# Work moved out of the routing blocks: turned tiles copied a step later, eight row buffers, router logits by groups, and the first expert weight slots split inside the normalisation before each mixture

## What is computed

```python
def _layernorm(x, axis=-1, eps=1e-05):
    m = jnp.mean(x, axis=axis, keepdims=True)
    v = jnp.var(x, axis=axis, keepdims=True)
    return (x - m) / jnp.sqrt(v + eps)
...
    x = x + _L0_ffn_ref(_layernorm(x, axis=-1), ...)   # logits = x @ Wg, softmax, top 2 of 8
    ...
    x = x + _L1_ffn_ref(_layernorm(x, axis=-1), ...)   # logits = x @ gate_w.T, sigmoid + bias, top 4 of 16
```

## Time and profile before

| what | us |
|---|---|
| median of 3 runs (lowest, highest) | 1519.88 (1517.51, 1522.65) |
| the profiled execution | 1531.23 |
| its span from first to last instruction | 1529.2 |
| boundary and route ahead of the first mixture | 517.8 to 575.3 |
| boundary and route ahead of the second mixture | 1099.4 to 1189.4 |

### The profile page before, as it was taken

One profiled execution on the slowest core, in us unless ns is written; L12 is line 12 of the kernel. 1 busy time (PEld: TensorE's weight loads), 2 busy tenths in 40 slices (PEclk: granted clock), 3 DMA queues, 4 the chain that ended last, 5 costly groups with the idle time before them and its releaser, 6 DMA issues. The chain is left out here.

```text
span 1529.2 us, 41178 instructions
## 1 busy us (share of the span) xinstructions
PE 1169.9 (77%) x13430; PEld 862.1 (56%) x13430; DVE 1031.0 (67%) x2885; ACT 826.0 (54%) x2163; POOL 435.7 (28%) x480
## 2 busy tenths in 40 slices
PE   4899999998798539999999927678723327787890
PEld 2688888886344429988888724235611215555660
DVE  5699999997647777966666545345779228454566
ACT  6688888885588546844444306127454125444450
POOL 0555555551200000023333202000200641555550
PEclk9999999999899759999999958789955659899895
DMA  2333333331000283011111169970160320222228
GB/s 95 99 78 80 82 76 81 81 82 64 1 1 1 91 318 155 2 57 47 51 50 51 37 204 321 348 234 1 66 255 28 87 65 19 73 76 78 78 69 281
DMA packets 111934, 151.45 MB, mean 99 GB/s; under 512 B 13632, under 2 KB 96960, under 8 KB 111680
## 3 DMA queue, kind: packets, MB, share of 16 engines
q1 hardware_dynamic: 95792, 114.11, 23.6%
q0 software_dynamic: 11328, 30.95, 6.6%
q10 hardware_dynamic: 4688, 4.72, 0.9%
HBM read 127.97 MB, written 21.76 MB: 98 GB/s over the span
## 5 line engine op out<-in xcount | busy, mean ns | idle before, releaser
L1291 ACT ACTIVATE mixture_and_attentions_h<-ps,mixture_and_attentions_b 128x128 f32<-128x128 f32 x440 | 125.3, 373 | 137.3 <-PE ps L1243 134.3
L1243 PE MATMUL ps<-xture_and_attentions_m_w 128*128 128x128 f16 x1872 | 156.2, 219 | 1.8 <-DVE xture_and_attentions_m_w L1319 1.7
L1243 PEld LDWEIGHTS ps<-xture_and_attentions_m_w 128*128 x1872 | 129.1, 98 | 37.1 <-issue 3.5
L648 POOL TENSOR_TENSOR ads_and_recurrence_ctx_s<-ads_and_recurrence_ctx_c,ads_and_recurrence_ctx_s 128x512 f16<-128x512 f32 x64 | 74.2, 1159 | 178.2 <-ACT ads_and_recurrence_ctx_s L577 178.2
L597 ACT ACTIVATE ads_and_recurrence_probs<-ps,s_and_recurrence_neg_max 128x257 f32<-128x257 f32 x256 | 117.7, 480 | 1.1 <-DVE s_and_recurrence_neg_max L679 1.1
L1261 PE MATMUL ps<-xture_and_attentions_m_w,ixture_and_attentions_hs 128*128 x312 | 117.5, 379 | 1.0 <-DVE xture_and_attentions_m_w L1344 1.0
L1599 POOL DMA_INDIRECT tage_second_mixture_rows<-n_rows,e_second_mixture_r_token x79 | 76.8, 973 | 133.7 <-POOLq L1002 110.0
L1475 PE MATMUL ps<-stage_second_mixture_m_w,stage_second_mixture_x_s 128*128 x474 | 98.5, 348 | 20.7 <-ACT stage_second_mixture_x_s L1517 13.9
L1603 POOL DMA_INDIRECT y_rows<-stage_second_mixture_y,ge_second_mixture_r_dest x79 | 77.1, 976 | 124.6 <-DVE stage_second_mixture_y L1571 114.5
L1371 POOL DMA_INDIRECT ture_and_attentions_rows<-n_rows,e_and_attentions_r_token x39 | 39.0, 999 | 258.1 <-POOLq L1002 159.6
L1327 DVE TENSOR_SCALAR ixture_and_attentions_hs<-mixture_and_attentions_h 128x512 f16<-128x512 f32 x110 | 47.6, 433 | 87.7 <-PE ps L1262 71.3
(11 more groups left out here) (401 smaller groups left out, 3371.9 us busy)
## 6 DMA issues: line engine op xcount, KB each, us to landing
ads_and_recurrence_ctx_t<-in_ctx_t SPq DMA_DIRECT2D x64, 257.0 KB, 2.7
e_and_attentions_b_ctx_t<-in_ctx_t SPq DMA_DIRECT2D x15, 1028.0 KB, 9.1
ure_and_attentions_b_ctx<-in_ctx SPq DMA_DIRECT2D x30, 512.0 KB, 8.9
xture_and_attentions_m_w<-in_m_w SPq DMA_DIRECT2D x2, 5632.0 KB, 37.3
ds_and_recurrence_mask_i<-in_mask SPq DMA_DIRECT2D x256, 32.1 KB, 1.7
tage_second_mixture_rows<-y_rows SPq DMA_DIRECT2D x16, 512.0 KB, 9.6
stage_second_mixture_m_w<-in_m_w SPq DMA_DIRECT2D x2, 3840.0 KB, 20.5
xture_and_attentions_m_w<-in_m_w SPq DMA_DIRECT2D x1, 5120.0 KB, 16.6
```

The costliest lines, as they stand in the source:

```text
L1243: last = pe.matmul(ps[:, UB + 2 * (u % 2) + f // PER, (f % PER) * P:(f % PER + 1) * P], slots.of(e, c, at, P), a[:, c, :], start=(n == 0), ...
L1291: last = act.activation(h32[n][:, at:at + P], ps[:, UB + 2 * (u % 2) + n, at:at + P], ACT.Silu, scale=1 / (WS * NS), bias=b1[:, bass.ds(e ...
```

## The change

Only boundaries with `rows=True` and what belongs to them are changed. ACT copies a pair of turned tiles one step later, and PE has four PSUM banks for them in place of two. There are eight row buffers in place of four, with eight semaphores for their stores. The logits are computed in the boundary, four tiles at a time, in the place where other boundaries have their projections (after the turns of steps 3, 5, 7 and 9). The first slots are split inside the boundary, on ACT in steps 5 to 8 and on DVE in steps 6 to 8 with one behind the last step. In the second mixture `early` falls from 5 to 3, so two more slots are split among the tiles: 14 slots over 12 tiles, two slots after tile 5 and two after tile 11.

```diff
-    PB, TB = 0, 2
+    PB, TB, AHEAD = (0, 0, 4) if b.rows else (0, 2, 2)
+    RB = 8 if b.rows else 4
...
             def turn(t):
                 pe.wait_ge(k.l_low.sem, k.l_low.at(t + 1))
-                pe.wait_ge(k.l_turned.sem, k.l_turned.at(t - 1))
-                out = ps[:, TB + t % 2, 0:D].bitcast(F16)
+                pe.wait_ge(k.l_turned.sem, k.l_turned.at(t - AHEAD + 1))
+                out = ps[:, TB + t % AHEAD, 0:D].bitcast(F16)
...
-                act.wait_ge(k.l_turn.sem, k.l_turn.at(t - 3))
-                if b.rows and t >= 4:
-                    act.wait_ge(k.x_rows[t % 4].sem, k.x_rows[t % 4].at(t // 4))
+                act.wait_ge(k.l_turn.sem, k.l_turn.at(t - RB + 1))
+                if b.rows and t >= RB:
+                    act.wait_ge(k.x_rows[t % RB].sem, k.x_rows[t % RB].at(t // RB))
...
-                if 0 < s <= H:
+                if b.rows and 1 < s <= H + 1:
+                    turned(2 * s - 4)
+                    turned(2 * s - 3)
+                if not b.rows and 0 < s <= H:
                     turned(2 * s - 2)
                     turned(2 * s - 1)
+                if b.slots and 5 <= s < 5 + b.slots.mix.early:
+                    b.slots.cast_high(act, s - 5)
...
+                if b.slots and 6 <= s < 6 + b.slots.mix.early:
+                    b.slots.cast_low(dve, s - 6)
+            if b.slots:
+                for i in range(H - 5, b.slots.mix.early):
+                    b.slots.cast_low(dve, i)
...
-MIX1 = Mixture(1, E1, K1, 1, 2 * C * I1 + 2 * D, P, 5, (3, 5, 11, 17), 1.0)
+MIX1 = Mixture(1, E1, K1, 1, 2 * C * I1 + 2 * D, P, 3, (3, 5, 11, 17), 1.0)
...
+def logits(k, mix, wg):
+    def project(pe, g, part):
+        if part == 0:
+            for t in range(4 * g, 4 * g + 4):
+                products = [(w, x, c) for w, x in three(wg, (k.n_h, k.n_l)) for c in range(C)]
+                for n, (w, x, c) in enumerate(products):
+                    last = pe.matmul(k.ps[:, 7, t * mix.E:(t + 1) * mix.E], x[:, c, t * P:(t + 1) * P], w[:, c, :], start=(n == 0), stop=(n == len(products) - 1))
+            if g == G - 1:
+                last.then_inc(k.m_logits.sem, 1)
+    return project
...
         def _(act):
-            for i in range(mix.early):
-                slots.cast_high(act, i)
             scores(act)
...
-            for i in range(mix.early):
-                slots.cast_low(dve, i)
             choose(dve)
...
         def casts(u):
-            return range(mix.early + u, mix.early + u + 1) if mix.early + u < mix.count else ()
+            rest, tiles = mix.count - mix.early, NT - 4
+            return range(mix.early + rest * u // tiles, mix.early + rest * (u + 1) // tiles) if u < tiles else ()
```

More of the change, by code:

```diff
@@ L1034, in _ @@
         def _(pe):
-            for t in range(NT):
-                products = [(w, x, c) for w, x in three(wg, (k.n_h, k.n_l)) for c in range(C)]
-                for n, (w, x, c) in enumerate(products):
-                    last = pe.matmul(ps[:, LB, t * E:(t + 1) * E], x[:, c, t * P:(t + 1) * P], w[:, c, :], start=(n == 0), stop=(n == len(products) - 1))
-            last.then_inc(k.m_logits.sem, 1)
             pe.wait_ge(k.m_counted.sem, k.m_counted.at(1))
@@ L1682, in stage_first_mixture_and_attentions @@
             slots = Slots(k, mix, ctx)
-            boundary(k, Boundary(weights, rows=True, fetch=fetch_ahead))
+            boundary(k, Boundary(weights, project=logits(k, mix, k.w["L0_ffn_Wg"]), rows=True, fetch=fetch_ahead, slots=slots))
             route_first(k, mix, slots, r)
@@ L1719, in choose @@
                 dve.tensor_tensor(r.w[:, n, :], ex[:, :, n], z[:, 3, :], ALU.mult)
-        route(k, mix, k.w["L0_ffn_Wg"], slots, scores, choose, r)
+        route(k, mix, slots, scores, choose, r)
 class Ring:
@@ L2142, in stage_second_mixture @@
             slots = Slots(k, mix, ctx)
-            boundary(k, Boundary(weights, rows=True, fetch=lambda sp: slots.fetch(sp, (0,))))
+            boundary(k, Boundary(weights, project=logits(k, mix, k.w["L1_ffn_gate_w_t"]), rows=True, fetch=lambda sp: slots.fetch(sp, (0,)), slots=slots))
             route_second(k, mix, slots, r)
@@ L2363, in build @@
         k.t_raw = [k.count(f"t_raw{p}", unit=16) for p in range(4)]
-        k.x_rows = [k.count(f"x_rows{p}", unit=16) for p in range(4)]
         k.ctx_t_loaded = [k.count(f"ctx_t{p}", unit=16) for p in range(Ring.SLOTS)]
@@ L2367, in build @@
         k.g_load = [k.count(f"g_load{p}", unit=16) for p in range(4)]
+        k.x_rows = [k.count(f"x_rows{p}", unit=16) for p in range(4)] + k.g_load
         k.t_rows = [k.count(f"t_rows{p}", unit=16) for p in range(8)]
```

34 lines of the change are left out of this document (17 added, 17 removed).

## The result

| | kernel before | changed kernel |
|---|---|---|
| median of 20 runs each | 1523.83 us | 1512.22 us |
| lowest, highest | 1517.51, 1529.71 | 1502.51, 1518.71 |
| ratio | 1 | 0.9927 (95% interval 0.9910 to 0.9944) |
| profiled execution (its span) | 1531.23 (1529.2) | 1517.76 (1515.8) |

The change saves 11.1 us, 8.5 to 13.7. The forecast was -11.2 us. The kernel before now has more runs and a median 4 us above the one that the prediction started from, so the difference is compared and not the absolute time.

A forecast was written before the change was run, and what follows sets the result against it. The prediction took DVE to set the boundaries' pace, with slots and a transfer wait delaying the route blocks. It summed -4.85 - 9.2 + 2.8 = -11.2 us, from 1519.9 to 1508.7 us, range 1501 to 1517.

The forecast's parts named there:

- Boundary steps: In both boundaries: steps without DVE's wait take 2.28 us in place of 2.54, and ACT's store wait costs nothing.
- End of the boundary: ACT's last copies and PE's logits, not the store, close the boundaries, 0.4 us later in the first, 0.2 in the second.
- the delay by the first slot: First boundary, steps 5 and 6: ACT ends its first slot 4.1 us after step 5 starts, making low 5.3, not 4.6.
- First route block: First mixture: DVE has only its constants left, 0.55 us, before reading the logits, in place of 5.80; 5.25 us saved.
- Second route block: Second mixture: DVE's first choice step comes 1.75 us in, in place of 11.17; 9.4 us saved.
- Two extra slots: Second tile block, tiles 5 and 11 behind the gathers: each extra slot costs 1.40 us of DVE, 2.8 us lost.
- Gathers: Head of second tile block: 44 gathers take the same 55 us, two slots under them, and engines resume as they end.
- 0.3 us for each slot: Second tile block: a slot's DVE work under the gathers delays a gather by 0.3 us; unchanged in number, adding nothing.
- (a): Rival, boundary: high, low and slot halves wait for each other, 7.6 us back, 1516.3 us; chance 0.10.
- (b): Rival, gather stretch: two tile periods fall behind it, 1514.2 us (chance 0.12), or two more under it, 1501.8 (further 0.10).
- (c): Rival: stall behind gathers grows as instructions arrive later; slower above 11.2 us of additional wait; chance 0.05.
- (d): Rival, boundaries: eight buffers or the later copy bring nothing, as waits only move; 1514.7 us; chance 0.03.

The follow-up runs named there:

- e1: Kernel before with only the later copies of turned tiles and the eight row buffers; 1515.92 us, ratio 0.9951.
- e3: Changed kernel with the early slots split at the head of the route blocks again, logits still in the boundary; 1516.80 us, ratio 0.9958 to the kernel before.
- e2: Kernel before with only early 3 in place of 5 in the second mixture and its 14 slots over 12 tiles; 1522.78 us, ratio 0.9994.
- e8: Kernel before, unchanged, profiled a second time; 1530.92 us.
- e11: Kernel before with later copies, eight buffers and gathers paced by DVE's results, 12 ahead; 1425.05 us, ratio 0.9943, kernel before 1434.48 on that chip.
- e4: Changed kernel with the old order: copies in their own step, two banks, four row buffers; 1525.19 us against 1524.13 of the kernel before.
- e5: Changed kernel with 24 gathers in a row in place of 44, the other 55 later; 1521.14 us against 1530.23 of the kernel before, ratio 0.9946.
- e6: Changed kernel with 44 gathers, after the first 12 POOL waiting for PE before every second one; 1493.60 us against 1530.23 of before, ratio 0.9757.
- e12: Changed kernel with gathers paced by DVE's results, six ahead, rerun on a slower chip; 1486.61 us against 1528.40 of the kernel before, ratio 0.9727.
- e9: Changed kernel with gathers paced by DVE's results, 12 ahead, two per tile; 1420.31 us, ratio 0.9902, kernel before 1434.48 on that chip.
- e10: Changed kernel with gathers paced by DVE's results, six ahead, mean 2.4 per tile; 1419.64 us, ratio 0.9896, kernel before 1434.48 on that chip.

## Why the prediction was right, point by point

**Boundary steps.** 2.28 us forecast, 2.27 measured, without the wait for the store. With the order alone this is worth 4.2 and 4.1 us (e1), of which my sum never wrote a number, because it priced only the end with the slots. The slots and the logits take 3.9 and 3.8 of it back (changed kernel against e1).

**End of the boundary.** The closing by ACT's copies and PE's logits was right, the size was not: -0.3 twice in place of +0.4 and +0.2. The term that was too large is the delay by the first slot. The working has ACT done with it 4.1 us behind the step's start and the low half 0.7 late; ACT was done after 3.9 (529.62 to 533.50), since its copies and slots take 0.95 each, and DVE waited 0.46. What follows was carried along: the last low half ended at 541.0 where the working gives 541.6.

**First route block.** DVE read the logits 0.33 us in, not 0.55; the saving was 5.4 for 5.25. e3 shows that the slots on DVE were the whole of it and the place of the logits none.

**Second route block.** 1.71 us for 1.75, and 9.5 for 9.4. e2 splits it: 5.3 from early 3 (two slots and the transfer), 4.2 from moving the other three. Against e8's 62.7 us it is 8.4 and 4.2: how long the kernel before waits for the transfer varies.

**Two extra slots.** Right in place, the size in doubt. Their tile periods are 4.2 us (results of tiles 5 and 6 at 1246.7 and 1250.9), the pair on DVE is one row:

```profile
1265.02 2.88 DVE L976 SCALAR_TENSOR_TENSOR stage_second_mixture_m_w<-stage_second_mixture_m_w 128x1280 f16<-128x1280 f32 x2
...
1268.11 2.10 PE L1492 MATMUL ps<-stage_second_mixture_m_w,stage_second_mixture_x_s 128*128 x6 [4.12 <-DVE stage_second_mixture_m_w L976]
```

and PE's wait for the last slot grew from 2.8 to 4.1. On the chips with the stall the kernels that have them fall 2.9 to 6.7 us short of their stages, so +2.8 is at the low end; what could cost more than twice 1.4, the traces do not say. From the first profile of before, the other terms are -15.5 where the sum had -14.0, and the two errors nearly cancel; from the second they are -14.0, and the change falls short by 2.9, both as forecast. The runs do not decide between the two, and the measured gain has an interval of 8.5 to 13.7 us: that 11.2 met 11.1 so closely is luck either way.

**Gathers.** 44 of them in 55.5 us, as forecast. Three slots of ACT stood under them, not two, and two of DVE. The prediction lets the engines resume as the gathers end; a tile's result came 4.4 us behind the last gather's start, and 7.6 in the kernel before. The two gathers that started under DVE's slots took 1.20 and 1.29 us, the others 0.95 to 1.04:

```profile
1189.34 0.95 POOL L1616 DMA_INDIRECT tage_second_mixture_rows<-n_rows,e_second_mixture_r_token  x1 [0.30 <-issue]
1190.59 1.20 POOL L1616 DMA_INDIRECT tage_second_mixture_rows<-n_rows,e_second_mixture_r_token  x1 [0.30 <-issue]
```

The prediction's 0.3 us for each slot is not a constant. DVE's slot here ran from 1189.48 to 1190.96, and the gather ended 0.82 behind it, at 1191.79. In the fourteen profiles 86 gathers start under a low half of 1.48 us, at least 0.2 us ahead of its end, and every one ends 0.81 or 0.82 us behind that low half. So such a gather takes 1.09 us when it starts 1.2 us into the slot, and 2.27 when it starts 0.05 into it (e11).

**The rivals.** (a) was the right mechanism for the wrong kernel: with the old order ACT does serialise the boundary and takes the whole gain (e4), with the new one it does not. (b) did not show beyond the block's variation of up to 8 us (331.6 to 339.8). (c), a stall that grows, did not happen; but that the stall belongs to POOL's row of transfers, which it supposed, is shown by e5 and e6. That it is instructions that arrive late is not shown: the trace gives "issue" and "remote" for the same stretch, the packets of the gathers take as long on the chip without the stall (0.16 and 0.17 us on average), and I found no run that tells late instructions from late semaphores. One row speaks against late instructions. The changed kernel's trace has a packet of the kind "instruction" 4.3 us into the block (1.14 us long) and one 17.2 us into it (0.35), and then none until 71.2, though the engines resume at 59.6. Whether these two queues serve every engine, the trace does not say. (d) is refuted by e1 and e4.

The Trainium skill (Runtime: NRT & Kernel Launch, on instruction fetch mechanics) holds that crossing a block of instructions is mostly hidden. The single waits of 23 us contradict it only if they are waits for instructions, and no run here shows that they are.

## What to carry to other kernels

Work moved into another stage pays by the idle time of the engine that sets the pace there: first free the pace (copies that wait for nobody, buffers enough that no store is awaited), then fill it; here the new order alone gave 7.5 us, the rest without it nothing that was measured, and both 11. Put work that hides into the stretch where engines stand anyway, and read where that stretch ends before work is laid behind it. And when engines stand for "issue" or an unknown queue beside a long row of gathers, pace the gathers by the consumer's progress: two added lines brought the gain here from 11 to 37 (e6) and 42 us (e12), and on the chip without the stall, where e9 and e10 ran, the whole was worth 14 to 15.

## What the runs showed of the hardware that I had not expected

- The kernel before takes 1524 to 1530 us on some chips and 1434 on another, in the one session that ran there. e10 and e12 are one kernel on the two kinds: their spans are 1420.6 and 1487.7 us, and 65.6 of the 67.1 us between them lie in the block with 79 gathers and 79 scatters (243.4 and 309.0 us). The stages up to it agree within their variation. The kernel before was not profiled on the other chip, so where its 90 us lie is inferred from this.
- On the slower kind, beside an unbroken row of gathers, PE, ACT and DVE stand for up to 23.2, 17.2 and 19.5 us at a time (ACT 27.8 in the kernel before). Two gathers in each tile of 2.76 us let the tiles keep their pace (e6); at 2.4 a tile, with six in a row, PE stood 4.97 us (e12).
- A gather that starts while DVE splits a slot ends 0.82 us behind that slot (all 86 cases with 0.2 us or more of the slot left), and takes 1.09 to 2.27 us for it in place of 0.95.
- Gathers and scatters need 1.25 us of POOL each (0.95 and 0.30 between two), 197.5 us for the 158 of this block. Where nothing else stalls, that is the block's bound: e9's last result comes at 198.3 us.
